# Attention of a fused two-layer kernel: the query norm as a row of the band, squares summed by feature, short products in one group

## The chip, the cores and the metric

The kernel runs on one core of one Trainium2 chip. The metric is the device time of one execution in microseconds. The engines are named as the profile names them: PE (TensorE, matmul), PEld (its weight load), DVE (VectorE), ACT (ScalarE), POOL (GpSimd) and SP (SyncE, which here only issues transfers). SBUF is the working memory, PSUM the eight banks into which PE writes, DRAM the memory off the core.

## The reference, cut to what matters

Four sub-layers over 4 x 512 tokens of width 512 (pooled attention, dense FFN, lag attention, experts), each followed by a layer norm. The change touches only the third, lag attention with 16 heads of 128:

```python
q, k, v = _silu(x @ Wq), _silu(x @ Wk), _silu(x @ Wv);  z = x @ Wz;  a = x @ Wa;  b = x @ Wb
q, k, v = (_causal_dwconv(t, conv) for t in (q, k, v))          # 4 taps along the sequence
q = q * cos + rot_half(q) * sin;  k = k * cos + rot_half(k) * sin
q = q / max(norm(q), 1e-12);  k = k / max(norm(k), 1e-12)       # per token and head
for s in range(4):                                              # lags 0 to 3
    attn = sum(q * lag(k, s)) * scale;  gate = sigmoid(lag(a, s) * b)
    out = out + (attn * gate) * lag(v, s)
rms = rsqrt(mean(out * out over all heads) + EPS)               # per token
out = out * rms * norm_w * _silu(z);  return out @ Wout
```

The norm of q is one factor per token and head. It can be applied to the scores, or, since it is linear, as late as the output's rows. All products are made in float32 by parts: a high part and a low part, three matmuls for one (`product`, lines 45 to 47).

## The kernel before, in words

The lag attention is a software pipeline of 64 steps, one for each head and batch (step s: head s // 4, batch s % 4). Every slot of the loop works on step f (the newest), l1, l2 and l3 (one, two and three steps older). There is no scheduler: the code of each engine is written out by hand, in the order in which it runs, and semaphores (`wait_ge`, `until`) tie the engines together. `BAND` is 131 columns: a tile of 128 keys and the 3 queries behind it.

In one slot PE makes four projections of 12 matmuls each (q and k mixed by halves into A and B, v into A, z into B), the output projection of l2 (4 tiles of 3 matmuls), and five groups of four short ones: it turns the convolved values (`turn_values`, into bank T), makes the scores (`score`, rot_k against rot_q over the band, into S), the mixture (`mix`, values against prob, into O), turns the mixture (`turn_mixed`, into T) and turns the squares of q and k (`turn_tiles(S1, squares[0])`). The short ones stand in two places: values and scores before the first half of the output projection, the other three before its second half.

DVE makes the convolutions (`tap`, three for each of c1, c2, cv), the rotation (cross1, cross2, r1, r2), the sums of squares per token (line 3405), `gains` (gate + 1, times the constant band matrix), `probabilities` (gate times scores), `gated_output`, `y_low` and `accumulate` (adds an output tile to the row in x_tok, times the query norm `rnorm`). ACT makes silu, the zeroth taps, squares, the gates (tanh), the values scaled by the key norm, and `sum_squares` (squares of the turned mixture, summed by the accumulator, times the query norm). POOL makes c1 * cos, c2 * cos, the sum of the two squares, the power -1/2 of the norms (line 3017) and, in three of four slots, the low parts of the next head's weights (`split_head`, lines 2885 and 2888: two of them, two, one). SP issues the gate row (line 2012), the next head's weights, and the four transfers that move the halves of r1 and r2 to rot_q and rot_k (lines 2098 to 2102), which `score` waits for a slot later.

Of the kernel before, what the change touches and what calls it, by code (L numbers as in the profile page):

```python
# [15 lines left out]
P = 128  # L16
# [1766 lines left out]
class Step:  # L1783


    def __init__(self, s):
        self.s, self.head, self.b = s, s // BATCH, s % BATCH
        self.wbuf, self.ybuf, self.rbuf = self.head % 2, s % 2, s % 4


def layers(nc, mem, a, lag_b, saved, store):
# [16 lines left out]
    with phase(nc) as ctx:  # L1808
# [19 lines left out]
        raw1 = overlay("second", [(None, 3 * MAT, F32), ("raw1", 8 * Paired.BLOCK, F32)])["raw1"]  # L1828
        exact = overlay("exact", [(None, 3 * MAT, F32), ("n40", 2 * SEQ, F32), (None, 4 * MAT - 2 * SEQ, F32), ("n41", 2 * SEQ, F32)])
# [6 lines left out]
        lag_a, ssum, expert_weight = small("lag_a", NTT * HEADS), small("ssum", NTT * HEADS), small("expert_weight", NTT * EXPERTS)  # L1836
# [11 lines left out]
        with ExitStack() as room:  # L1848
# [17 lines left out]
                      + [("gate", TPB * BAND, F32), ("mixed", SEQ, F32), ("prob", TPB * BAND, F32),  # L1866
                         ("rot_q", SEQ + PAD, F32), ("values", SEQ, F32), (None, 3 * SEQ - 2 * TPB * BAND - PAD, F32),
                         ("zs", SEQ, F32), ("wo_hi1", HID, F32R), ("wo_lo1", HID, F32R), ("b_row", SEQ + PAD, F32),
                         ("band", BAND, F32), ("conv", HEADS * 3 * LAGS, F32), ("norm", HEADS, F32),
                         ("norm2", 2 * TPB, F32)] + [(f"rnorm{r}", 2 * TPB, F32) for r in range(4)])  # L1870
# [46 lines left out]
        gate, mixed, prob, rot_q, values = banded(lag["gate"]), lag["mixed"], banded(lag["prob"]), lag["rot_q"], lag["values"]  # L1917
        b_row, zs, band_t, conv_t, norm_t = (lag[n] for n in ("b_row", "zs", "band", "conv", "norm"))
        norm2, rnorm = lag["norm2"], [lag[f"rnorm{r}"] for r in range(4)]
# [49 lines left out]
        s_cos, s_cross = sem("cos"), sem("cross")  # L1969
        s_r1, s_r2 = sem("r1"), sem("r2")  # L1970
        s_move1, s_move2 = sem("move1"), sem("move2")
        s_sqr, s_pair = sem("sqr"), sem("pair")
        s_nrm, s_sum, s_n2, s_rn = sem("nrm"), sem("sum"), sem("n2"), sem("rn")
        s_b, s_gate, s_gain = sem("b"), sem("gate"), sem("gain")
        s_s, s_prob = sem("s"), sem("prob")
        s_vt, s_val = sem("vt"), sem("val")
        s_o, s_mix, s_ot, s_osq = sem("o"), sem("mix"), sem("ot"), sem("osq")
        s_y, s_yhi, s_ylo = sem("y"), sem("yhi"), sem("ylo")
# [17 lines left out]
        SWITCH = END - 2  # L1996
# [3 lines left out]
        with nc.Block() as block:  # L2000
            @block.sync
            def _(sp):
# [7 lines left out]
                def factor_row(st):  # L2010
                    row = st.head + HEADS
                    sp.dma_start(b_row[:, 0:SEQ], lag_b[row:row + 1, st.b * SEQ:(st.b + 1) * SEQ]
                                 .to_broadcast([P, SEQ])).then_inc(s_b, 16)

# [53 lines left out]
                save(1)  # L2068
                factors.store(sp, 0)
# [3 lines left out]
                for f, l1, l2, l3 in slots():  # L2073
# [6 lines left out]
                    factor_row(f)  # L2080
                    if f.b == 0:
# [5 lines left out]
                    if f.s == END - 1:  # L2087
                        sp.wait_ge(s_save, BATCH * 16)
                        sp.wait_ge(s_op, (STEPS - BATCH) * TPB)
                        load_residual(0)  # L2090
# [5 lines left out]
                    sp.wait_ge(s_r1, f.s + 1)  # L2096
# [3 lines left out]
                    sp.wait_ge(s_r2, f.s + 1)  # L2100
# [36 lines left out]
            def _(pe):  # L2137
# [5 lines left out]
                def out_projection(st, tiles):  # L2143
# [3 lines left out]
                    for t in tiles:  # L2147
                        until(pe, s_acc, st.s * TPB + t - 1)
                        tok = slice(t * P, (t + 1) * P)
                        product(pe, OP[t % 2], [(y_hi[st.ybuf][:, tok], y_lo[st.ybuf][:, tok])],  # L2150
                                [(wo_hi[st.wbuf], wo_lo[st.wbuf])]).then_inc(s_op, 1)

                def score(st):
                    pe.wait_ge(s_move1, st.s * 32 + 32)
                    pe.wait_ge(s_move2, st.s * 32 + 32)
                    pe.wait_ge(s_sum, st.s + 1)
                    until(pe, s_prob, st.s)
# [5 lines left out]
                def mix(st):  # L2163
                    pe.wait_ge(s_prob, st.s + 1)
# [12 lines left out]

                def turn_values(st):
                    pe.wait_ge(s_cv, st.s * TAPS + TAPS)
                    until(pe, s_osq, st.s - 1 if st.s < SWITCH else st.s)  # L2180
                    turn_tiles(T, cv, s_vt)

                def turn_mixed(st):

                    pe.wait_ge(s_val, st.s + 2)
                    pe.wait_ge(s_mix, st.s + 1)
                    turn_tiles(T, mixed, s_ot)
# [94 lines left out]
                for f, l1, l2, l3 in slots():  # L2282
# [18 lines left out]
                    if l1:  # L2301
# [1358 lines left out]
```

## Time and profile before

| what | value |
|---|---|
| time, median of 3 runs | 2850.29 us (2849.97 to 2850.31) |
| profiled execution, first to last instruction | 2847.8 us (its own time is not recorded beside the span) |
| PE, PEld busy | 2826.6 us (99%), 2348.4 us (82%) |
| DVE busy | 2252.7 us (79%) |
| ACT, POOL busy | 1528.7 us (54%), 1443.2 us (51%) |
| granted TensorE clock, mean | 0.999 of full speed |
| transfers, mean | 56 GB/s |
| chain that ended last, PE's share | 32%, the rest in smaller pieces of other lines |

The span of the profiled execution lies 2.5 us under the median of the timed runs. A slot of the lag attention takes 16.8 us, and the loop of 64 slots lies between about 760 and 1850 us of the span. PE is busy nearly all the time in every stage; DVE is busy nine tenths of the time in the lag attention and less elsewhere. Busy time says what an engine does, not what it waits for; a timeline of one slot tells both.

### The profile page before, as it was taken

How to read it: one execution, taken by the hardware profiler on the slowest of the kernel's cores; microseconds unless marked ns; L12 is line 12 of the kernel's file. 1: busy time of each engine (PE TensorE's matmuls, PEld its weight loads, DVE VectorE, ACT ScalarE, POOL GpSimd, SP SyncE). 2: the span in 40 equal slices, each digit the busy share in tenths (PEclk: the TensorE clock that was granted, in tenths of full speed). 3: DMA queues.
4: the chain of work that ended last, by engine and by line, in shares of the span. 5: the costliest groups of instructions: out<-in, count | busy, mean ns of one | idle time of the engine just before them, and what ended most of it. 6: DMA issues, size and time to landing. Idle time of an engine off the chain costs nothing. (4 is left out here: it accounts for less than half of the span.)

```text
span 2847.8 us, 40066 instructions
## 1 busy us (share of the span) xinstructions
PE 2826.6 (99%) x13466; PEld 2348.4 (82%) x13466; DVE 2252.7 (79%) x3265; ACT 1528.7 (54%) x3149; POOL 1443.2 (51%) x1016
## 2 busy tenths in 40 slices
PE   9999999999999999999999999999999999999998
PEld 7888888888788888888888888778778887888887
DVE  7899587777888889888988898977667677666665
ACT  6656333333666666666666666765545445444443
POOL 7787233334344444444444444666545556555554
PEclk9999999999999999999999999999999999999999
DMA  3000000000322222222222221321111111211111
GB/s 138 1 23 25 12 19 27 30 27 23 125 65 68 70 64 64 65 73 64 64 64 72 77 71 53 93 75 52 52 45 52 60 45 56 86 45 60 52 52 45
DMA packets 79099, 160.44 MB, mean 56 GB/s; under 512 B 11313, under 2 KB 19889, under 8 KB 77873
## 3 DMA queue, kind: packets, MB, share of 16 engines
q1 hardware_dynamic: 78896, 157.88, 18.5%
q8 instruction: 110, 1.80, 0.3%
q14 instruction: 93, 0.75, 0.1%
HBM read 115.63 MB, written 8.65 MB: 44 GB/s over the span
## 5 line engine op out<-in xcount | busy, mean ns | idle before, releaser
L1546 DVE SCALAR_TENSOR_TENSOR x_tok<-OP,expert_weight,x_tok 128x512 f32<-128x512 f32 x252 | 188.1, 748 | 138.2 <-PE OP L47 138.1
L1425 POOL TENSOR_TENSOR middle_w_lo<-second_raw,middle_w_hi 128x512 fp32r<-128x512 f32 (+1 forms) x96 | 143.4, 1496 | 208.7 <-ACT middle_w_hi L1420 208.7
L1518 POOL TENSOR_TENSOR middle_in_lo<-middle_slot,middle_in_hi 128x512 fp32r<-128x512 f32 x128 | 168.6, 1318 | 131.7 <-ACT middle_in_hi L1514 130.9
L3017 POOL TENSOR_TENSOR lag_rnorm<-lag_norm,minus_half 128x8 f32<-128x8 f32 x64 | 105.1, 1643 | 209.5 <-DVE lag_norm L3408 209.5
L45 PE MATMUL B<-xT_hi,lag_w_hi 128*128 128x512 f32 x516 | 201.4, 390 | 1.8 <-DVE xT_lo L496 1.5
L47 PE MATMUL B<-xT_hi,lag_w_lo 128*128 128x512 f32 x516 | 201.6, 391 | 0.0
L45 PE MATMUL A<-xT_hi,lag_w_hi 128*128 128x512 f32 x512 | 200.6, 392 | 0.4 <-DVE xT_lo L496 0.4
L46 PE MATMUL B<-xT_lo,lag_w_hi 128*128 128x512 f32 x516 | 200.8, 389 | 0.0
L47 PE MATMUL A<-xT_hi,lag_w_lo 128*128 128x512 f32 x512 | 199.9, 390 | 0.0
L46 PE MATMUL A<-xT_lo,lag_w_hi 128*128 128x512 f32 x512 | 199.4, 389 | 0.0
L45 PE MATMUL OP<-middle_down_hi,middle_in_hi 128*128 128x512 f32 x496 | 193.6, 390 | 1.9 <-POOL middle_down_lo L1445 1.7
L47 PE MATMUL OP<-middle_down_hi,middle_in_lo 128*128 128x512 f32 x496 | 193.0, 389 | 0.0
L46 PE MATMUL OP<-middle_down_lo,middle_in_hi 128*128 128x512 f32 x496 | 193.0, 389 | 0.0
L3086 DVE SCALAR_TENSOR_TENSOR lag_c<-A,lag_conv,lag_c 128x511 f32<-128x511 f32 (+2 forms) x192 | 143.8, 749 | 60.4 <-ACT lag_c L2694 55.9
L1425 POOL TENSOR_TENSOR middle_w_lo<-middle_raw,middle_w_hi 128x512 fp32r<-128x512 f32 (+1 forms) x96 | 154.4, 1613 | 64.6 <-ACT middle_w_hi L1420 62.6
L3097 DVE SCALAR_TENSOR_TENSOR x_tok<-OP,lag_rnorm,x_tok 128x512 f32<-128x512 f32 x240 | 173.5, 744 | 2.9 <-PE OP L47 2.9
L1263 DVE TENSOR_TENSOR x_tok<-OP,x_tok 128x512 f32<-128x512 f32 x188 | 128.8, 688 | 54.7 <-PE OP L47 54.3
L3086 DVE SCALAR_TENSOR_TENSOR lag_c<-B,lag_conv,lag_c 128x511 f32<-128x511 f32 (+2 forms) x192 | 143.4, 747 | 25.2 <-ACT lag_c L2702 23.0
L3013 POOL TENSOR_TENSOR lag_r<-lag_c,lag_cos 128x512 f32<-128x512 f32 x64 | 83.5, 1305 | 155.4 <-DVE lag_c L3086 155.4
L3008 POOL TENSOR_TENSOR lag_r<-lag_c,lag_cos 128x512 f32<-128x512 f32 x64 | 83.0, 1296 | 153.1 <-DVE lag_c L3086 153.1
L1508 ACT ACTIVATE middle_slot<-middle_slot 128x512 f32<-128x512 f32 x128 | 80.8, 632 | 139.2 <-DVE middle_slot L1527 139.1
L3086 DVE SCALAR_TENSOR_TENSOR lag_cv<-A,lag_conv,lag_cv 128x511 f32<-128x511 f32 (+2 forms) x192 | 143.7, 748 | 12.8 <-ACT lag_cv L2720 2.0
(670 smaller groups left out, 9103.8 us busy)
## 6 DMA issues: line engine op xcount, KB each, us to landing
lag_raw<-in_head_weights SPq DMA_DIRECT2D x64, 256.0 KB, 4.5
lag_b_row<-lag_b_scratch SPq DMA_DIRECT2D x64, 256.0 KB, 3.3
lag_rot_q<-lag_r SPq DMA_DIRECT2D x128, 128.0 KB, 2.3
lag_rot_k<-lag_r SPq DMA_DIRECT2D x128, 128.0 KB, 2.4
middle_down_raw<-in_expert_down SPq DMA_DIRECT2D x32, 512.0 KB, 3.4
middle_raw<-in_expert_in SPq DMA_DIRECT2D x32, 384.0 KB, 3.0
second_raw<-in_expert_in SPq DMA_DIRECT2D x32, 384.0 KB, 3.0
double_raw<-in_dense_in SPq DMA_DIRECT2D x12, 512.0 KB, 3.4
```

What stands on the lines that cost most here:

```text
L45: pe.matmul(out, lh, rh, start=first and k == 0, stop=False)
L46: pe.matmul(out, lh, rl, start=False, stop=False)
L47: done = pe.matmul(out, ll, rh, start=False, stop=last and k == n - 1)
L1263: dve.tensor_tensor(row, self.down_bank(q, n), row, ALU.add).then_inc(self.s_acc, 1)
L1425: pool.tensor_tensor(self.w_lo[q % 2][:, out], self.raw[q % 2][:, of], f32(self.w_hi[q % 2][:, out]), ALU.subtract).then_inc(self.s_wlo, 1)
L1518: pool.tensor_tensor(self.inner_lo[q % 3][t], self.slot((1, 3)[t], q), f32(self.inner_hi[q % 3][t]), ALU.subtract).then_inc(self.s_lo, 1)
L1546: dve.scalar_tensor_tensor(row, self.down_bank(v, n), self.expert_weight[:, e:e + 1], row, op0=ALU.mult, op1=ALU.add).then_inc(self.s_acc, 1)
L3008: pool.tensor_tensor(r1, c1, cos, ALU.mult).then_inc(s_cos, 1)
L3013: pool.tensor_tensor(r2, c2, cos, ALU.mult).then_inc(s_cos, 1)
L3017: pool.tensor_tensor(rnorm[f.rbuf], norm2, half[:, 0:2 * TPB], ALU.pow).then_inc(s_rn, 1)
L3086: dve.scalar_tensor_tensor(out[:, shift:], src[:, 0:SEQ - shift], wj, out[:, shift:], op0=ALU.mult, op1=ALU.add).then_inc(done, 1)
L3097: dve.scalar_tensor_tensor(row, OP[t % 2], at(rnorm[st.rbuf], 2 * t), row, op0=ALU.mult, op1=ALU.add).then_inc(s_acc, 1)
```

## The change

The query norm no longer scales the output rows, it scales the probabilities. The norms of a step lie with tokens in partitions (128 x 8). DVE turns them in blocks of 32x32 (`turn_norms`), five small stores write them to DRAM as a row for each tile (`store_query`), one load spreads the row over all partitions (`load_query`, 128x524), POOL multiplies it by the band matrix (`band_of_query`), and `probabilities` multiplies the gate by that. `gains` now takes the scores from PSUM in place of the band. The probabilities and `mix` are made one slot later (for l2), `accumulate` is a plain add, the power on POOL stands ahead of c1 * cos.

The turned mixture and `sum_squares` are gone but for the last two steps. ACT squares the mixture as it takes it from PSUM (`mixture`, Square), POOL adds it by an accumulating transfer into DRAM, one region per batch (`add_squares`), and PE turns each region once at the end (`turn_sums`). PE makes all short products of a slot in one group (squares, values, mixture, scores) and all four tiles of the output projection behind one another, into OP0, OP1, S0 and S1. The turned squares go to OP1.

```diff
+                def store_query(st):
+                    sp.wait_ge(s_n2, 3 * st.s + 3)
+                    until(sp, s_query, st.s * 96)
+                    window = query_norm[st.s % 2, :, :]
+                    for g in range(TPB):
+                        sp.dma_start(window[:, g * 32:(g + 1) * 32], turned[g * 32:g * 32 + TPB, :]).then_inc(s_query, 16)
+                    sp.dma_start(window[0:TPB - 1, P:BAND], turned[1:TPB, 0:PAD]).then_inc(s_query, 16)
+
+                def load_query(st):
+                    sp.wait_ge(s_query, st.s * 96 + 80)
+                    until(sp, s_prob, 2 * st.s)
+                    sp.dma_start(lag["query"], query_norm[st.s % 2:st.s % 2 + 1, :, :].rearrange("a t n -> a (t n)")
+                                 .to_broadcast([P, TPB * BAND])).then_inc(s_query, 16)
...
                     if l1:
+                        turn_squares(l1)
                         turn_values(l1)
+                        if l2:
+                            mix(l2)
                         score(l1)
-                    if l2:
-                        if l2.s == 0:
-                            pe.wait_ge(factors.s_c, BATCH)
-                        out_projection(l2, (0, 1))
...
                         projection(l1, 3, B, s_z)
-                        if f.s < SWITCH:
-                            if l2:
-                                turn_mixed(l2)
-                            mix(l1)
...
-                    turn_tiles(S1, squares[0], s_nrm)
...
+                    if l2:
...
+                        out_projection(l2, range(TPB), [OP0, OP1, S0, S1], 4)
...
+                def band_of_query(st):
+                    pool.wait_ge(s_query, st.s * 96 + 96)
+                    pool.tensor_tensor(query[:, :, :], query[:, :, :], band_t.unsqueeze(1).to_broadcast([P, TPB, BAND]),
+                                       ALU.mult).then_inc(s_band, 1)
+
+                def add_squares(st):
+                    pool.wait_ge(s_mix, st.s + 1)
+                    if st.s < WHOLE:
+                        until(pool, s_squares, st.s * 16)
+                        sums = square_sums[st.b * P:(st.b + 1) * P, :]
+                        if st.head:
+                            pool.dma_start(sums, head_out[st.s], accum_op=ALU.add).then_inc(s_squares, 16)
...
                 def gains(st):
                     dve.wait_ge(s_gate, st.s + 1)
-                    dve.scalar_tensor_tensor(gate[:, :, :], gate[:, :, :], 1.0,
-                                             band_t.unsqueeze(1).to_broadcast([P, TPB, BAND]),
-                                             op0=ALU.add, op1=ALU.mult).then_inc(s_gain, 1)
+                    dve.wait_ge(s_s, st.s + 1)
+                    dve.scalar_tensor_tensor(gate[:, :, :], gate[:, :, :], 1.0, scores[:, :, 0:BAND],
+                                             op0=ALU.add, op1=ALU.mult).then_inc(s_prob, 1)
 
                 def probabilities(st):
-                    dve.wait_ge(s_s, st.s + 1)
-                    dve.wait_ge(s_gain, st.s + 1)
+                    dve.wait_ge(s_prob, 2 * st.s + 1)
                     until(dve, s_o, st.s)
-                    dve.tensor_tensor(prob[:, :, :], gate[:, :, :], scores[:, :, 0:BAND], ALU.mult).then_inc(s_prob, 1)
+                    if st.s < BY_ROW:
+                        dve.wait_ge(s_band, st.s + 1 + (st.s > WHOLE))
+                        dve.tensor_tensor(prob[:, :, :], gate[:, :, :], query[:, :, :], ALU.mult).then_inc(s_prob, 1)
...
+                def turn_norms(st):
+                    dve.wait_ge(s_rn, st.s + 1)
+                    until(dve, s_query, st.s * 96)
+                    dve.transpose(turned, norms[st.rbuf]).then_inc(s_n2, 1)
```

On PE, in the middle of the loop, the short products of one slot. Before, from the end of the z projection on (`lag_mixed` is the mixture, `lag_cv` the values, `lag_square` the squares):

```order
L47 MATMUL B<-xT_hi,lag_w_lo 128x512
L2175 MATMUL T<-ident,lag_mixed 128x128 x4
L2169 MATMUL O<-lag_prob,lag_values 128x131 x3
L2169 MATMUL O<-lag_prob,lag_values 128x128
L2175 MATMUL S<-ident,lag_square 128x128 x4
```

and now, between the second and the third projection:

```order
L47 MATMUL B<-xT_hi,lag_w_lo 128x512
L2216 MATMUL OP<-ident,lag_square 128x128 x4
L2216 MATMUL T<-ident,lag_cv 128x128 x4
L2210 MATMUL O<-lag_prob,lag_values 128x131 x3
L2210 MATMUL O<-lag_prob,lag_values 128x128
L2200 MATMUL S<-lag_rot_q,lag_rot_k 128x131 x4
L45 MATMUL A<-xT_hi,lag_w_hi 128x512
```

The turned mixture is gone, and the values and scores, which had a place of their own, stand in the same group.

On POOL, one slot of the loop with weight splits. Before:

```order
L2885 TENSOR_TENSOR lag_w_lo<-lag_raw,lag_w_hi 128x512 x2
L3008 TENSOR_TENSOR lag_r<-lag_c,lag_cos 128x512
L3013 TENSOR_TENSOR lag_r<-lag_c,lag_cos 128x512
L3015 TENSOR_TENSOR lag_square<-lag_square 128x512
L3017 TENSOR_TENSOR lag_rnorm<-lag_norm,minus_half 128x8
```

and now (`square_sums_scratch` is the region in DRAM to which the mixture's squares are added; the slot shown is one with a single split):

```order
L2952 TENSOR_TENSOR lag_query<-lag_query,lag_band 128x524
L2944 TENSOR_TENSOR lag_w_lo<-lag_raw,lag_w_hi 128x512
L3082 TENSOR_TENSOR lag_norms<-lag_norm,minus_half 128x8
L3085 TENSOR_TENSOR lag_r<-lag_c,lag_cos 128x512
L2961 DMA square_sums_scratch<-head_squares 128x512
L3090 TENSOR_TENSOR lag_r<-lag_c,lag_cos 128x512
L3092 TENSOR_TENSOR lag_square<-lag_square 128x512
```

The band product and the issue of the transfer are new, and the power has moved from the end to the front, so that c1 * cos comes after it.

On DVE, the part of a slot from the sums of squares to the rotation, as it stands now (before, each cross product stood directly behind the convolution or the probabilities, and the sums of squares at the end of the slot):

```order
L3214 TENSOR_REDUCE lag_norm<-OP 128x4x2
L3217 TENSOR_SCALAR lag_norm<-lag_norm 128x8
L3167 SCALAR_TENSOR_TENSOR lag_c<-B,lag_conv,lag_c 128x511
L3204 SCALAR_TENSOR_TENSOR O<-O,lag_norm,lag_zs 128x512
L3167 SCALAR_TENSOR_TENSOR lag_c<-B,lag_conv,lag_c 128x510
L3167 SCALAR_TENSOR_TENSOR lag_c<-B,lag_conv,lag_c 128x509
L3188 SCALAR_TENSOR_TENSOR lag_gate<-lag_gate,S 128x524
L3222 STREAM_TRANSPOSE lag_turned<-lag_norms 128x32
L3209 TENSOR_TENSOR lag_y_lo<-O,lag_y_hi 128x512
L3480 TENSOR_TENSOR lag_cross<-lag_c,lag_sin 128x512
L3486 TENSOR_TENSOR lag_cross<-lag_c,lag_sin 128x512
```

Both cross products stand together now, behind the turn of the norms and y_low.

## Rows read from the trace of the kernel before

**Rows 1.** Windows; us, then busy time of each engine, clock, DMA share, GB/s

```profile
800.00:1780.00 980.00, 980.00 (x5139) 833.44 (x5138) 877.43 (x1343) 624.59 (x1643) 416.95 (x305) 1.00 0.25 67
1780.00:1880.00 100.00, 97.96 (x486) 76.07 (x485) 84.87 (x141) 74.11 (x178) 59.34 (x52) 1.00 0.31 93
```

**Rows 2.** Timeline of PE in one slot; start, us, line, out<-in, count

```profile
1105.89 0.60 PE L2175 MATMUL T<-ident,lag_mixed 128*128 128x128 f32 x4
1106.33 1.06 PE L2169 MATMUL O<-lag_prob,lag_values 128*128 128x131 f32 x8
1107.23 0.60 PE L2175 MATMUL S<-ident,lag_square 128*128 128x128 f32 x4
1107.58 0.48 PE L45 MATMUL OP<-lag_w_hi,lag_y_hi 128*128 128x512 f32 x1
...
1114.48 0.60 PE L2175 MATMUL T<-ident,lag_cv 128*128 128x128 f32 x4
1114.92 1.06 PE L2159 MATMUL S<-lag_rot_q,lag_rot_k 128*128 128x131 f32 x8
1115.74 0.48 PE L45 MATMUL OP<-lag_w_hi,lag_y_hi 128*128 128x512 f32 x1
1116.05 0.40 PE L46 MATMUL OP<-lag_w_lo,lag_y_hi 128*128 128x512 f32 x1
...
1122.65 0.60 PE L2175 MATMUL T<-ident,lag_mixed 128*128 128x128 f32 x4
```

**Rows 3.** Timeline of DVE in the same slot; idle time before, in brackets

```profile
1108.19 0.75 DVE L3115 SCALAR_TENSOR_TENSOR O<-O,lag_norm,lag_zs 128x512 f32<-128x512 f32 x1
1108.85 0.68 DVE L3405 TENSOR_REDUCE lag_norm<-S 128x8 f32<-128x512 f32 x1
1109.57 0.17 DVE L3408 TENSOR_SCALAR lag_norm<-lag_norm 128x8 f32<-128x8 f32 x1
...
1113.44 2.32 DVE L3086 SCALAR_TENSOR_TENSOR lag_c<-A,lag_conv,lag_c 128x511 f32<-128x511 f32 x3 [0.87 <-ACT lag_c L2694]
1116.10 0.75 DVE L3086 SCALAR_TENSOR_TENSOR lag_c<-B,lag_conv,lag_c 128x511 f32<-128x511 f32 x1 [0.35 <-ACT lag_c L2702]
1116.77 0.69 DVE L3110 TENSOR_TENSOR lag_prob<-lag_gate,S 128x524 f32<-128x524 f32 x1
1117.37 0.69 DVE L3360 TENSOR_TENSOR lag_cross<-lag_c,lag_sin 128x512 f32<-128x512 f32 x1
1117.97 1.53 DVE L3086 SCALAR_TENSOR_TENSOR lag_c<-B,lag_conv,lag_c 128x510 f32<-128x510 f32 x2
1119.42 1.40 DVE L3097 SCALAR_TENSOR_TENSOR x_tok<-OP,lag_rnorm,x_tok 128x512 f32<-128x512 f32 x2
...
1121.52 2.32 DVE L3086 SCALAR_TENSOR_TENSOR lag_cv<-A,lag_conv,lag_cv 128x511 f32<-128x511 f32 x3
1123.75 0.68 DVE L3394 TENSOR_TENSOR lag_r<-lag_r,lag_cross 128x512 f32<-128x512 f32 x1
```

**Rows 4.** Timeline of POOL in the same slot

```profile
1109.82 1.65 POOL L3017 TENSOR_TENSOR lag_rnorm<-lag_norm,minus_half 128x8 f32<-128x8 f32 x1 [3.21 <-DVE lag_norm L3408]
1111.67 2.63 POOL L2885 TENSOR_TENSOR lag_w_lo<-lag_raw,lag_w_hi 128x512 fp32r<-128x512 f32 x2 [0.21 <-ACT lag_w_hi L2442]
```

**Rows 5.** Tile view, expert stage; durations in ns, min/median/max

```profile
L1537 DVE TENSOR_TENSOR middle_slot<-middle_slot x64: 682/1762/1773, 1880.5 to 2827.5; 128x512 f32<-128x512 f32 x64
```

**Rows 6.** Timeline of POOL, expert stage

```profile
1897.95 1.41 POOL L1518 TENSOR_TENSOR middle_in_lo<-middle_slot,middle_in_hi 128x512 fp32r<-128x512 f32 x1 [1.30 <-ACT middle_in_hi L1514]
```

**Rows 7.** Timeline of DVE, same place

```profile
1898.24 1.40 DVE L1406 TENSOR_TENSOR middle_raw<-middle_raw 128x256 f32<-128x256 f32 x1
```

**Rows 8.** SP's issues of the gate row; ns each, min/median/max

```profile
L2012 SPq DMA_DIRECT2D lag_b_row<-lag_b_scratch x64: 325/332/585, 765.1 to 1819.4; - x64
```

**Rows 9.** Transfers of 1060 to 1160 us; count, KB, median us from issue to landing

```profile
lag_b_row<-lag_b_scratch SPq DMA_DIRECT2D x6, 256.0 KB, 3.2
```

**Rows 10.** The four 64 KB stores into lag_b_scratch, issue to landing

```profile
DMA to landing us min/median/max: 1.6/2.7/3.5
```

More of the change, by code:

```diff
@@ L1828, in layers @@
         raw1 = overlay("second", [(None, 3 * MAT, F32), ("raw1", 8 * Paired.BLOCK, F32)])["raw1"]
+        of_batch = overlay("sums", [(None, MAT, F32)] + [(f"rows{b}", SEQ, F32) for b in range(BATCH)])
         exact = overlay("exact", [(None, 3 * MAT, F32), ("n40", 2 * SEQ, F32), (None, 4 * MAT - 2 * SEQ, F32), ("n41", 2 * SEQ, F32)])
@@ L1916, in layers @@
         c1, c2, cv, rot_k, squares = lag["c1"], lag["c2"], lag["cv"], lag["rot_k"], [lag["square0"], lag["square1"]]
-        gate, mixed, prob, rot_q, values = banded(lag["gate"]), lag["mixed"], banded(lag["prob"]), lag["rot_q"], lag["values"]
+        gate, prob, rot_q, values = banded(lag["gate"]), banded(lag["prob"]), lag["rot_q"], lag["values"]
+        query = banded(lag["query"])
+        sum_rows = [of_batch[f"rows{b}"] for b in range(BATCH)]
+        head_out = {**{s: head_squares for s in range(STEPS - 3)}, END - 2: lag["query"][:, 0:SEQ],
+                    END - 1: lag["query"][:, 0:SEQ], END: squares[1]}
         b_row, zs, band_t, conv_t, norm_t = (lag[n] for n in ("b_row", "zs", "band", "conv", "norm"))
-        norm2, rnorm = lag["norm2"], [lag[f"rnorm{r}"] for r in range(4)]
+        norm2, norms, turned = lag["norm2"], [lag["norms0"], lag["norms1"]], lag["turned"]
         residual = [[middle[f"res{g}{t}"] for t in range(TPB)] for g in range(BATCH)]
@@ L1977, in layers @@
         s_o, s_mix, s_ot, s_osq = sem("o"), sem("mix"), sem("ot"), sem("osq")
+        s_query, s_band = sem("query"), sem("band")
+        s_squares, s_rows = sem("squares"), sem("rows")
         s_y, s_yhi, s_ylo = sem("y"), sem("yhi"), sem("ylo")
@@ L2760, in _ @@
                 rows.high_tile(act, 3)
+                mixture(last_step)
                 rows.copy(act, 0)
@@ L3355, in _ @@
                         norm1.aggregate(dve, 3)
+                    if l2:
+                        gated_output(l2)
+                    tap(1, f, B, c2, 2, s_c2)
+                    tap(1, f, B, c2, 3, s_c2)
+                    if l1:
+                        gains(l1)
+                        if f.s == END:
+                            probabilities(l1)
+                            sum_features(2, OP0)
+                        turn_norms(l1)
+                    if f.s == 1:
+                        factors.take(dve, 3, 3)
@@ L3356, in _ @@
+                    if l2:
+                        y_low(l2)
                     dve.wait_ge(s_c1, f.s * TAPS + TAPS)
[L3357 removed]
+                    until(dve, s_rotated, 4 * f.s)
                     if f.s == 0:
                         dve.wait_ge(s_rotation, 32)
[L3360 to L3363 removed]
@@ L3385, in _ @@
+                    until(dve, s_rotated, 4 * f.s - 1)
+                    dve.tensor_tensor(cross1, c2, sin, ALU.mult).then_inc(s_rotated, 1)
+                    dve.wait_ge(s_tap, f.s * 3 + 3)
+                    tap(2, f, A, cv, 1, s_cv)
                     tap(2, f, A, cv, 2, s_cv)
@@ L3427, in _ @@
                 accumulate(before_last, 1)
-                rows.low_tile(dve, 0)
-                for t in (1, 2, 3):
+                for t in range(TPB):
                     rows.low_tile(dve, t)
```

357 lines of the change are left out of this document (195 added, 162 removed).

## The prediction

> **What bounds the kernel now.** I read the windows first. In the loop of the lag attention PE is busy 980.00 of 980 us at full clock, DVE 877.43, ACT and POOL far less [rows 1]. So PE sets the time, and what counts is how far apart its instructions start. The timeline of PE shows that: one slot runs from 1105.89 to 1122.65, 16.76 us [rows 2]. From 1116.05 to the next turned mixture stand 29 wide matmuls in 6.60 us, 0.228 each. Four turns cost 0.44 us behind a wide matmul (1105.89 to 1106.33) and 0.35 behind short ones (1107.23 to 1107.58); the mixture costs 0.90, the scores 0.82, and the first wide matmul behind a short group 0.31 in place of 0.228 [rows 2].
>
> The timeline of DVE shows how near the next bound is. By the starts, a tensor_tensor takes 0.60 us, the gated output 0.66, the sums of squares 0.72, three convolution taps 2.23, two of them 1.45, one 0.67; the idle pieces of 0.87 and 0.35 are waits for ACT [rows 3]. DVE rests under 2 us in a slot.
>
> **PE's part.** Before, the short work is 0.44 + 0.90 + 0.35 + 0.08 and 0.44 + 0.82 + 0.08 = 3.11 us a slot. Now it is one group: squares 0.44, values 0.35, mixture 0.90, scores 0.82, and 0.08 behind it, 2.59. PE needs 16.24 us a slot, 0.52 less: 0.35 is the turned mixture, the rest is the second entry and exit. Some 60 slots have the whole pattern: 31 us, if nobody makes PE wait.
>
> **DVE's part.** I write one slot from the start of the probabilities, with the durations of [rows 3]. Probabilities 0 to 0.60; taps of c1 to 2.83; sums of squares to 3.55; maximum 0.17, to 3.72; a tap of c2 to 4.39; gated output to 5.05; two taps to 6.50; gains, now with PSUM, 0.65, to 7.15; the 32x32 turn, which no row shows, between the 0.17 of the smallest instruction and 0.60 of a 512-wide one: 128x32 is nearest to 0.17, to 7.32; y_low to 7.93; cross2 to 8.53; cross1 to 9.13; cv to 11.36; r1, r2 to 12.56; four accumulates, plain adds now, at 0.60 in place of about 0.66 (1119.42 to the next cross product is 1.32 for two), to 14.96. Sum 15.0 against PE's 16.24: free, by itself.
>
> **Who blocks whom.** In the expert stage a DVE product of two SBUF tiles takes 0.68 us at best and 1.76 in the median [rows 5]: it stands still while POOL runs. A POOL product takes 1.31 alone (2.63 for two, [rows 4]). At 1897.95 one takes 1.41, and the DVE product issued behind it at 1898.24 takes 1.40 although it is half as wide as the other, whose least is 0.68 [rows 6, 7]. I read this as an exclusive right, given in the order of asking, for a whole instruction. In the loop before the cross products show none of it (0.69, [rows 3]): no POOL product runs there. The Trainium skill states the same limit ("SBUF — State Buffer", Who interferes with whom): only a DVE instruction with two SBUF inputs meets a POOL instruction that reads SBUF, one with a PSUM input does not. By that rule, with which the stretched rows agree, the probabilities are newly exposed: gate times scores read PSUM, gate times query reads SBUF twice.
>
> *Cross products.* POOL starts the power 0.08 behind the maximum, at 3.80, ends it at 5.45 (1.65, [rows 4]), makes c1 * cos to 6.75, issues the adding transfer, and makes c2 * cos and the sum of squares. No row shows a transfer that POOL issues. From below: what SP takes for one, 0.33 to 0.59 [rows 8]. From above: 2.6, two POOL products. The nearest rows for something POOL has to work out for 128 partitions are its product, 1.31, and its power, 1.65 [rows 4]; I take 1.3 to 1.65. Then c2 * cos asks between 8.05 and 8.40, while cross2 (7.93 to 8.53) runs; it gets the port at 8.53, and cross1 waits until 9.84. Cost 1.3 us; DVE's slot is 16.3. The thresholds: under 1.18 us c2 * cos comes ahead of cross2, and both cross products are held (1.4 to 2.5 us); over 1.78 neither, at most 0.4. The Trainium skill gives about 1 us to the first byte for a transfer issued by POOL ("DMA: Bandwidth & Descriptors", Specifications); no run here shows it. As an estimate by that page the issue would fall under the threshold, with the time of the second rival below.
>
> *Probabilities.* SP sees the turned norms at 7.35. Five small stores start 0.37 to 0.63 apart (issue 0.33 to 0.59 [rows 8] and 0.04 between); at 0.45 the last starts at 9.15. The four 64 KB stores landed in 1.6 to 3.5 us, median 2.7 [rows 10]; here it is under 0.6 KB, so I take 1.6: 10.75. SP is blocked meanwhile; behind it wait the moves of r1 and r2, which are ready only past 12, so this costs nothing. The load is of the gate row's shape, 3.2 us [rows 9]: 13.98. Band product 1.31: 15.34 with the signals. POOL goes straight on to its weight splits in three of four slots, 1.31 each [rows 4], two, two and one. DVE asks at 16.3, the first split ends at 16.65: 0.35 us in three slots of four, 0.26 on average. The slot is 16.56.
>
> So PE waits for DVE (the third projection for c2, the first of the next slot for cv), and of its 0.52 us 0.20 remain: 12 us over 60 slots.
>
> **The rest.** ACT loses the turned squares and gains nothing; it rests anyway [rows 1]. The adding transfer has a slot to land. The end of the loop gets four sums of 512 columns by feature on DVE (0.68 each, the duration in [rows 3], 2.7 us), four turned regions on PE (0.44 each) and their loads; PE rests 2.04 us there now [rows 1]. Between 0 and 8 us lost; I take 2, since the other work there covers part.
>
> **Sum.** The profiled execution's span is 2847.8 us; 12 less and 2 more make 2837.8, and with the 2.5 us by which the median of the runs lies above that span, 2840. 0.2% is 5.7 us, what a measurement of this kernel can tell from no change.
>
> **Rivals.**
>
> *PE stays the bound.* The issue on POOL lasts past 1.78 us, or the held products fall into DVE's slack, and the row comes in time. Against it: the probabilities wait for the band at 15.34 and are held by a split. Even then DVE's slot is at most 16.65 in three slots and 15.34 in one, 16.3 on average, PE's 16.24. For it: PE never waits today. 0.46 to 0.52 us by 60 less 2 us: 2821 to 2825.
>
> *Slower: both cross products held.* The issue on POOL takes under 1.18 us, say 0.7. c2 * cos takes the port at 7.45, cross2 waits to 8.76, the sum of squares asks meanwhile and goes ahead of cross1: 2.1 us a slot, DVE at 17.1; the second split (16.65 to 17.96) holds the probabilities for 0.86 us in two slots of four. 17.5 against 16.76: 46 us more, 2896 to 2898. It decides from 1.18 us down. For it: SP's 0.33 to 0.59. Against it: POOL's own rows.
>
> *Slower: the row is late.* At a landing of 2.7 and 0.6 between the stores the band product ends at 17.0, a split holds the probabilities to 18.3 in three slots of four: 18.0 on average, 1.24 by 60, 75 us, and half of that at half the delay; 2889 to 2927.
>
> *The sizes cancel.* A collision a little larger, or an end 5 us dearer: within 0.2%.
>
> **Chances.** Forecast 0.35, of which 0.30 lie below 2844.6 and 0.05 within 0.2%; its own range is 2828 to 2850. PE bound 0.24. Both held 0.23. Row late 0.10. Cancelled 0.08. So faster 0.54, same 0.13, slower 0.33. The range goes from 2820, under the first rival, to 2898, which leaves out most of the late row and little more.
>
> **What would show it.** PE: the turned mixtures gone, one group of 16 short products in about 2.5 us; its idle time before the third projection and before the first, put down to taps on DVE. DVE: cross1 near 1.9 us and cross2 near 0.69 is my forecast; both long is the slower rival; both 0.69 the faster. Probabilities near 1.0 us where splits follow, 0.69 in every fourth slot. POOL: the space between c1 * cos and c2 * cos is the issue. SP: five stores, then the load; if DVE's idle time ahead of the probabilities is put down to the band product, the late row decides. I am wrong if DVE's slot is not the sum of these, or if PE waits for a move or the gate instead.

## The result, and the profile after

The changed kernel takes 2918.9 us (median of 4 runs, 2917.2 to 2920.1) against 2850.3: 1.024 of the time before, 95% interval 1.0226 to 1.0254. It is 2.4% slower. I had forecast 2840, with 0.33 for slower, and the time lies outside my range as well.

The page of the changed kernel (busy time and share; then groups: busy us, mean ns | idle time before them):

```profile
PE 2824.5 (97%) x13234; PEld 2324.3 (80%) x13234; DVE 2393.1 (82%) x3332; ACT 1449.4 (50%) x2653; POOL 1586.8 (54%) x1140
L45 PE MATMUL A<-xT_hi,lag_w_hi 128*128 128x512 f32 x512 | 211.6, 413 | 61.7 <-DVE lag_cv L3167 61.3
```

Its windows, as in [rows 1], and two from the end of the loop:

```profile
800.00:1780.00 980.00, 924.80 (x4655) 764.63 (x4653) 955.01 (x1330) 524.29 (x1124) 522.94 (x403) 1.00 0.40 94
1890.00:1900.00 10.00, 5.32 (x24) 4.58 (x22) 9.93 (x22) 2.25 (x6) 1.99 (x2) 0.64 0.59 159
1900.00:1910.00 10.00, 7.29 (x29) 5.98 (x30) 5.89 (x11) 7.03 (x14) 8.80 (x9) 0.67 0.18 53
```

The bound has changed hands: DVE is busy 955 of 980 us, and PE, which never waited in [rows 1], rests 55 us, 48 of them ahead of the first projection, until the last tap of cv is made. The mean slot is 17.68 us, where it was 16.81 (60 slots each, from the first silu of the second step to that of the 62nd). The last step starts 53.5 us later than before; the other 15.7 us of the profiled difference (span 2917.0 against 2847.8) lie behind that start, 13.4 of them ahead of the first matmul of the experts.

The timeline of DVE in one slot, to be read beside [rows 3]:

```profile
1206.31 0.17 DVE L3217 TENSOR_SCALAR lag_norm<-lag_norm 128x8 f32<-128x8 f32 x1
1209.76 0.20 DVE L3222 STREAM_TRANSPOSE lag_turned<-lag_norms 128x32 f32<-128x32 f32 x1
1209.89 0.65 DVE L3209 TENSOR_TENSOR lag_y_lo<-O,lag_y_hi 128x512 fp32r<-128x512 f32 x1
1210.46 3.01 DVE L3480 TENSOR_TENSOR lag_cross<-lag_c,lag_sin 128x512 f32<-128x512 f32 x1
1213.39 0.68 DVE L3486 TENSOR_TENSOR lag_cross<-lag_c,lag_sin 128x512 f32<-128x512 f32 x1
1213.99 2.31 DVE L3167 SCALAR_TENSOR_TENSOR lag_cv<-A,lag_conv,lag_cv 128x511 f32<-128x511 f32 x3
1219.81 1.83 DVE L3196 TENSOR_TENSOR lag_prob<-lag_gate,lag_query 128x524 f32<-128x524 f32 x1
```

and that of POOL:

```profile
1206.56 1.67 POOL L3082 TENSOR_TENSOR lag_norms<-lag_norm,minus_half 128x8 f32<-128x8 f32 x1 [3.67 <-DVE lag_norm L3217]
1208.21 1.28 POOL L3085 TENSOR_TENSOR lag_r<-lag_c,lag_cos 128x512 f32<-128x512 f32 x1
1209.45 0.88 POOL L2961 DMA_DIRECT2D square_sums_scratch<-head_squares  x1
1210.10 1.56 POOL L3090 TENSOR_TENSOR lag_r<-lag_c,lag_cos 128x512 f32<-128x512 f32 x1
1211.36 1.54 POOL L3092 TENSOR_TENSOR lag_square<-lag_square 128x512 f32<-128x512 f32 x1
1217.28 1.29 POOL L2952 TENSOR_TENSOR lag_query<-lag_query,lag_band 128x524 f32<-128x524 f32 x1 [4.37 <-DMA lag_query<-query_norm_scratch]
```

I read the record of a held product as running from where its engine asks for it to its end. cross2 is asked at 1210.46 and ends 0.6 us after the sum of squares does, although that sum starts 0.90 us later than cross2 asks; cross1 behind it is free. The issue of the transfer keeps POOL for 0.65 us (1209.45 to 1210.10), and the two products behind it are recorded 0.3 us into one another. Over 50 slots (ns, least/median/most):

```profile
L3480 DVE TENSOR_TENSOR lag_cross<-lag_c,lag_sin x50: 2546/2942/3034, 911.0 to 1775.3; 128x512 f32<-128x512 f32 x50
L3486 DVE TENSOR_TENSOR lag_cross<-lag_c,lag_sin x50: 676/679/683, 913.9 to 1778.2; 128x512 f32<-128x512 f32 x50
L3196 DVE TENSOR_TENSOR lag_prob<-lag_gate,lag_query x50: 696/699/1839, 902.8 to 1766.5; 128x524 f32<-128x524 f32 x50
```

Of these 50 probabilities 10 are held for a whole product of POOL (1.13 us), 6 more for under 0.5 us. The slot's sum: from one start of the probabilities to the next 18.20 us here, less the two holds (3.01 - 0.68 and 1.84 - 0.70) leave 14.73 of DVE's own. Over the 60 slots cross2's mean hold is 2.23 us and that of the probabilities 0.28, and DVE rests 0.48; together 17.72, against 17.68 measured.

### The profile page after: what moved, and what is told of

Read it like the earlier page. It is cut to its first block, busy times and chain, and to the rows that moved or that the text cites. A ratio compares the mean times of both kernels' runs of the same rounds, so it can differ in the third digit from the quotient of the medians.

```text
span 2917.0 us, 39883 instructions
## 1 busy us (share of the span) xinstructions
PE 2824.5 (97%) x13234; PEld 2324.3 (80%) x13234; DVE 2393.1 (82%) x3332; ACT 1449.4 (50%) x2653; POOL 1586.8 (54%) x1140
## 3 DMA queue, kind: packets, MB, share of 16 engines
q8 instruction: 108, 1.77, 0.3%
## 4 chain that ended last, share of the span: by engine, by line
PE 60%; DVE 29%; issue 6%; ACT 3%; DMA 1%; POOL 1%; SPq 0%; DVEq 0%; ACTq 0%; POOLq 0%
PE OP L45 7%; PE OP L47 6%; PE OP L46 6%; DVE lag_c L3167 6%; DVE lag_cross L3480 6%; DVE lag_cv L3167 4%; PE S L1470 3%; PE S L1472 3%; PE S L1471 3%; PE A L45 2%; PE A L1470 2%; PE A L1472 2%; PE A L1471 2%; PE A L47 2%; PE A L46 2%
## 5 line engine op out<-in xcount | busy, mean ns | idle before, releaser
L45 PE MATMUL A<-xT_hi,lag_w_hi 128*128 128x512 f32 x512 | 211.6, 413 | 61.7 <-DVE lag_cv L3167 61.3
L3082 POOL TENSOR_TENSOR lag_norms<-lag_norm,minus_half 128x8 f32<-128x8 f32 x63 | 105.0, 1667 | 244.3 <-DVE lag_norm L3217 244.3
L2952 POOL TENSOR_TENSOR lag_query<-lag_query,lag_band 128x524 f32<-128x524 f32 x62 | 84.6, 1364 | 263.6 <-DMA lag_query<-query_norm_scratch 263.6
L2748 ACT ACTIVATE A<-A 128x512 f32<-128x512 f32 x64 | 37.2, 582 | 342.1 <-PE A L47 342.1
L3480 DVE TENSOR_TENSOR lag_cross<-lag_c,lag_sin 128x512 f32<-128x512 f32 x64 | 179.5, 2804 | 0.0
L45 PEld LDWEIGHTS A<-xT_hi,lag_w_hi 128*128 128x128 f32 x512 | 96.0, 188 | 103.4 <-DVE lag_cv L3167 62.8
L1470 PE MATMUL S<-xT_hi,middle_w_hi 128*128 128x512 f32 x384 | 150.4, 392 | 1.5 <-ACT middle_slot L1503 0.8
```

The source lines that it names most:

```text
L45: pe.matmul(out, lh, rh, start=first and k == 0, stop=False)
L1470: pe.matmul(out, w_hi, hi[:, k, :], start=first and k == 0, stop=False, skip_group_check=not first)
L3480: dve.tensor_tensor(cross2, c1, sin, ALU.mult).then_inc(s_rotated, 1)
```

## The experiments

My theory after the result: the holds of cross2 and of the probabilities by POOL, and nothing of the row's way through DRAM, cost the loop its 53.5 us, and the end is a cost of its own. The rivals: the row is late, or the transfers' own traffic slows DVE. Ten kernels followed.

| kernel | cross2, cross1 (median us) | mean slot | time, us | against before, 95% |
|---|---|---|---|---|
| before | 0.69, 0.69 | 16.81 | 2850.3 | |
| after | 2.94, 0.68 | 17.68 | 2918.9 | 1.0226 to 1.0254 |
| x1, no row | 3.91, 1.77 | 20.75 | 3103.8 | 1.0875 to 1.0907 |
| x2, products wait | 0.68, 0.68 | 16.77 | 2862.7 | 1.0025 to 1.0053 |
| x3, splits wait too | 0.68, 0.68 | 16.36 | 2838.9 | 0.9947 to 0.9973 |
| x4, transfer last | 0.77, 1.77 | 16.62 | 2854.0 | 1.0003 to 1.0022 |
| x5, x3 and the end | as x3 | 16.42 | 2839.1 | 0.9951 to 0.9976 |
| x6, only splits wait | 2.92, 0.68 | 17.56 | 2909.0 | 1.0194 to 1.0222 |
| x7, x4 and splits wait | 0.76, 1.78 | 16.50 | 2847.3 | 0.9981 to 0.9999 |
| x8, y_low later | 3.48, 0.68 | 19.94 | 3055.4 | 1.0703 to 1.0735 |
| x9, pause for transfer | 1.50, 1.78 | 17.49 | 2910.1 | 1.0194 to 1.0229 |
| x10, transfer first | 3.00, 0.68 | 18.15 | 2949.6 | 1.0334 to 1.0369 |

**x1.** SP's stores and load are gone, and POOL's band product multiplies band by band, so it waits for nothing; the norms are left out of the result.

```diff
-                        store_query(l1)
-                        load_query(l1)
...
-                    pool.wait_ge(s_query, st.s * 96 + 96)
-                    pool.tensor_tensor(query[:, :, :], query[:, :, :], band_t.unsqueeze(1).to_broadcast([P, TPB, BAND]),
+                    until(pool, s_prob, 2 * st.s)
+                    pool.tensor_tensor(query[:, :, :], band_t.unsqueeze(1).to_broadcast([P, TPB, BAND]), band_t.unsqueeze(1).to_broadcast([P, TPB, BAND]),
```

> The five stores of the norms as a row and the load that spreads them are left out, and the band product multiplies the band by itself, so the query norm is missing from the output; all else stands. Theory A (the SBUF port: cross2 is held 2.3 us behind two POOL products, DVE's own work of 15.0 us and this hold set the slot): the slot stays near 17.3 us, cross2 near 2.9 us, the probabilities go to 0.69 us everywhere since the weight splits are over by then; 2895 to 2905 us. Theory B (the row's way through DRAM sets the slot): without it the slot falls to PE's 16.24 us, and the time to about 2835 us.

3103.8 us: both missed. Without the wait for the row, POOL runs from the transfer through three products without a break. POOL, and the cross product under it, in one slot:

```profile
1317.50 0.89 POOL L2959 DMA_DIRECT2D square_sums_scratch<-head_squares  x1
1318.16 1.56 POOL L3088 TENSOR_TENSOR lag_r<-lag_c,lag_cos 128x512 f32<-128x512 f32 x1
1319.41 1.55 POOL L3090 TENSOR_TENSOR lag_square<-lag_square 128x512 f32<-128x512 f32 x1
1320.65 1.32 POOL L2950 TENSOR_TENSOR lag_query<-lag_band 128x524 f32<-128x524 f32 x1
```

```profile
1318.60 3.93 DVE L3477 TENSOR_TENSOR lag_cross<-lag_c,lag_sin 128x512 f32<-128x512 f32 x1
```

cross2 is held over all three. In 29 of 43 slots a weight split stands behind the band product, but starts 0.03 to 0.4 us after its end; there DVE got its turn first, and cross1, asked behind that, was held by the split (1.77 us). In one slot POOL asked for the split 0.21 us before the band product ended, and cross2 was held over four products, with cross1 free (0.68):

```profile
1716.39 1.30 POOL L2950 TENSOR_TENSOR lag_query<-lag_band 128x524 f32<-128x524 f32 x1
1717.48 1.45 POOL L2941 TENSOR_TENSOR lag_w_lo<-lag_raw,lag_w_hi 128x512 fp32r<-128x512 f32 x1
```

```profile
1714.24 5.26 DVE L3477 TENSOR_TENSOR lag_cross<-lag_c,lag_sin 128x512 f32<-128x512 f32 x1
```

PE waits 1.4 to 3.4 us a slot, and its granted clock falls to a mean of 0.91 between 1000 and 1600 us, which makes the slot longer still. The wait for the row had been a shield: it kept the band product off the rotation.

**x2 and x3.** POOL's second product waits for both cross products; in x3 the weight splits also wait for the probabilities.

```diff
                     until(pool, s_move2, f.s * 32)
+                    pool.wait_ge(s_rotated, 4 * f.s + 2)
                     pool.tensor_tensor(r2, c2, cos, ALU.mult)
...
+                        if l2 and l2.s < BY_ROW:
+                            pool.wait_ge(s_prob, 2 * l2.s + 2)
                         split_head(f.head + 1, 1 - f.wbuf, SPLIT_AT[f.b])
```

> One wait more: POOL starts c2 * cos only when DVE has made both cross products. The adding transfer and its traffic stay. Theory A (port): cross2 falls from 2.9 to 0.69 us, the slot from 17.6 to about 16.9 us, because now the row's way binds (15.9 us from turn to turn, and 1.15 us more where a weight split holds the probabilities, in three slots of four); about 2874 us. Rival C (the cross product is slowed by the transfer that POOL issues just ahead of it, not by POOL's products): cross2 stays near 2.9 us and the time near 2919 us.

> The wait of x2, and a second: POOL starts the weight splits only when DVE has made the probabilities. Theory A: no two-input DVE product meets a POOL product any more except perhaps r1; probabilities and cross products near 0.69 us, the slot 16.24 us, bound by PE as counted in the prediction; about 2835 us with the dearer end of the loop (16 us) as it is in the changed kernel. Theory B (late row): the slot stays over 16.8 us and DVE rests ahead of the probabilities, 2870 us or more.

x2 takes 56 us off (2862.7, where 2874 was expected), and x3 another 24 (2838.9, against 2835), which is 0.4% under the kernel before, with all of the change in it. Both transfers are still there, so traffic on them isn't what made cross2 long. x3's cross2 and probabilities, and its short products on PE, which answer to [rows 2]:

```profile
L3483 DVE TENSOR_TENSOR lag_cross<-lag_c,lag_sin x54: 678/681/685, 899.5 to 1765.5; 128x512 f32<-128x512 f32 x54
L3199 DVE TENSOR_TENSOR lag_prob<-lag_gate,lag_query x54: 703/705/2215, 907.7 to 1774.5; 128x524 f32<-128x524 f32 x54
```

```profile
1219.98 0.60 PE L2216 MATMUL OP<-ident,lag_square 128*128 128x128 f32 x4
1220.42 0.60 PE L2216 MATMUL T<-ident,lag_cv 128*128 128x128 f32 x4
1220.86 1.06 PE L2210 MATMUL O<-lag_prob,lag_values 128*128 128x131 f32 x8
1221.75 1.06 PE L2200 MATMUL S<-lag_rot_q,lag_rot_k 128*128 128x131 f32 x8
1222.57 0.47 PE L45 MATMUL A<-xT_hi,lag_w_hi 128*128 128x512 f32 x1
```

0.44 + 0.44 + 0.89 + 0.82, and 0.08 in the first wide one: 2.67, where I had 2.59 (the values cost 0.44, not 0.35). PE is busy 979.44 of 980 us, the slot is 16.36. One product is still held, r1 by POOL's sum of squares (1.14 us in the median), and PE doesn't wait for it.

**x4.** The adding transfer is issued behind the sum of squares (`add_squares(l2)` moves two instructions down).

> Only the place of the adding transfer changes: POOL issues it behind the sum of the squares and no longer between c1 * cos and c2 * cos, so both products come 0.65 us earlier. If the port is given in the order of asking: cross2 near 0.8 us, cross1 near 2.0 us. If POOL keeps it for as long as its next product is ready: cross2 near 2.1 us, cross1 0.69. If the products overlapped by 0.3 us only because they stood behind the transfer, they go back from 1.56 to 1.29 us each. In all three cases the hold falls from 2.3 to about 1.4 us, the slot to about 16.9, the time to about 2875 us.

2854.0 us, where I had 2875. cross2, cross1, and POOL's sum of squares:

```profile
L3480 DVE TENSOR_TENSOR lag_cross<-lag_c,lag_sin x53: 709/765/867, 902.9 to 1764.2; 128x512 f32<-128x512 f32 x53
L3486 DVE TENSOR_TENSOR lag_cross<-lag_c,lag_sin x53: 1769/1774/1780, 903.6 to 1764.9; 128x512 f32<-128x512 f32 x53
L3090 POOL TENSOR_TENSOR lag_square<-lag_square x53: 1728/1732/1737, 903.1 to 1764.4; 128x512 f32<-128x512 f32 x53
```

Here the engines do take turns: cross2 goes behind c2 * cos, the sum of squares waits 0.44 for it, and cross1 waits for the sum. But two things had changed at once, what stood ahead of the products and the moment at which DVE asked. x8 to x10 separate them.

**x5.** x3 with the work behind the loop in another order.

```diff
+                    if f.s == END:
+                        accumulate(third, 0)
+                        accumulate(third, 1)
                     if f.s >= END - 1:
                         mean_squares(f.s - (END - 1))
...
-                for t in range(TPB):
-                    accumulate(third, t)
-                y_low(before_last)
+                accumulate(third, 2)
+                accumulate(third, 3)
                 statistics(0)
                 norm_2.aggregate(dve, 0)
                 norm_sums(last_step)
+                y_low(before_last)
                 sum_features(3, OP0)
...
-                pool.wait_ge(s_n2, 3 * END + 2)
-                pool.tensor_tensor(norms[last_step.rbuf][:, 0:2 * TPB], norm2, half[:, 0:2 * TPB], ALU.pow).then_inc(s_rn, 1)
                 mean_root(1)
                 norm_2.root(pool, 0)
+                pool.wait_ge(s_n2, 3 * END + 2)
+                pool.tensor_tensor(norms[last_step.rbuf][:, 0:2 * TPB], norm2, half[:, 0:2 * TPB], ALU.pow).then_inc(s_rn, 1)
```

> The version with both waits (2838.9 us), with the work behind the last step put in another order: DVE takes the third-last step's first two output tiles into the rows ahead of the two sums of the rotation, the statistics of the first rows ahead of the norm sums, and the last low half behind them; POOL takes the two small powers of the statistics ahead of the power of the last norm. Theory (the 14.5 us behind the last step are PE's four waits of 1.1, 2.6, 2.7 and 2.5 us there and the lower clock that follows on them): the second and third wait shrink by 3 to 5 us together, and if the clock stays at its high level another 5 to 7 us come back: 2829 to 2834 in all. Rival (the clock falls for another reason, or the waits move on to the next thing that DVE is late with): 2836 to 2839.

2839.1, no gain over x3. PE's longest waits there, x3 first, then x5 (sum, times, longest):

```profile
PE OP L45 <- DVE lag_norm L3220: 2.7, 1, 2.7
PE OP L2216 <- DVE x_tok L3182: 2.6, 1, 2.6
```

```profile
PE S L2200 <- DMA lag_rot_k<-lag_r: 3.1, 1, 3.1
PE OP L45 <- DVE ms L3229: 2.9, 1, 2.9
```

x3's third wait, 2.5 us ahead of the turns of x_tok (L945), is gone in x5. The others moved on: the accumulates ahead of the rotation's sums made these late, and the scores wait for their move. The clock still falls, for a shorter time: by the granted clock of 10 us rows, 13.6 us at the 1.2 GHz level in x3 (0.73 and 0.59 from 1810 to 1830) and 6.8 in x5 (0.66 from 1820 to 1830). From the last step's start to the end it is 1039.7 us in place of 1043.2 (before: 1028.6), but in this profiled execution that start is 4.9 us later, in steps whose order is the same in both; why, no run shows. For the time the rival holds.

**x6 and x7.** The splits' wait alone, in the changed kernel and in x4.

> The changed kernel with one wait alone: POOL begins the weight splits only when DVE has the product of gate and band (probabilities). The products of the rotation stay as they are. If the two costs add (both waits took 24 us more than the wait for the cross products alone): the probabilities at 0.70 us in every slot, cross2 still held at about 3 us, the slot about 17.35, and 2893 to 2900. Rival (the time saved at the probabilities is lost again at the cross products, as DVE then meets POOL at another moment): 2910 to 2919.

> The adding transfer behind the sum of squares, and the wait of the splits for the probabilities. cross2 at 0.7 to 0.87 us, cross1 held 1.1 us (one POOL product), the probabilities at 0.70. DVE's own work of 15.0 us and 1.2 us held give 16.2, at PE's 16.24, so PE is the bound: 2839 to 2845. Rival (the hold of cross1 comes ahead of the cv taps that PE waits for, and PE loses part of it each slot): about 2850.

x6 2909.0, x7 2847.3, both between my two readings. The probabilities are free in x6 (0.69 us in every slot), yet this gives 10 us and not 24. Two reasons are in the traces. They were held for a whole product in only 10 of 50 slots of the changed kernel, but in 39 of 52 of x2 (1.67 us in the median): with cross2 held, DVE comes later to the splits. And DVE's sum isn't the whole bound: in x6's slot at 1209 us the last tap of cv ends at 1212.65, PE makes the first projection, ACT silu and scale, and the taps of c1 start at 1217.24. That round takes 4.6 us, and DVE has 4.2 us of work for it, so a hold there is partly free.

**x8.** DVE's y_low goes behind both cross products, so that cross2 is asked 0.57 us earlier.

> The changed kernel with one DVE instruction moved: the low half of y (reads PSUM, 0.6 us) goes behind both cross products, from the third step on, so cross2 asks about 0.57 us earlier, some 0.2 us before POOL begins c2 * cos. If the right is given in the order of asking, cross2 takes 0.68 to 0.75 us, c2 * cos waits for it, and cross1, asked while c2 * cos runs, is held once (1.3 to 1.9 us in all): the slot loses about 1.2 us of its 17.6, 2845 to 2865. If what is held is held over both POOL products whenever they follow one another, cross1 takes 2.4 to 3.0 us, and the time is 2895 to 2919.

3055.4: both missed. POOL and then cross2 in one slot:

```profile
1217.73 0.87 POOL L2961 DMA_DIRECT2D square_sums_scratch<-head_squares  x1
1218.38 1.54 POOL L3090 TENSOR_TENSOR lag_r<-lag_c,lag_cos 128x512 f32<-128x512 f32 x1
1219.64 1.53 POOL L3092 TENSOR_TENSOR lag_square<-lag_square 128x512 f32<-128x512 f32 x1
```

```profile
1218.26 3.46 DVE L3480 TENSOR_TENSOR lag_cross<-lag_c,lag_sin 128x512 f32<-128x512 f32 x1
```

cross2 asks 0.12 us ahead of c2 * cos, while the transfer is being issued, and stands behind both products all the same. The order of asking is refuted here: 0.12 us is little where POOL's records overlap by 0.3, but the sum of squares starts 1.38 us after cross2 has asked and still goes first, as it did in the changed kernel. The time is more than this hold: y_low now starts 4.0 us later in DVE's order (cross1 and the held cross2), PE waits 2.0 to 2.4 us a slot for it ahead of the output products, and its mean clock over the span falls to 0.969.

**x9.** x4 with a power of two columns on POOL where the transfer had been.

```diff
                     if l2 and l2.s < BY_ROW:
-                        add_squares(l2)
+                        pool.wait_ge(s_rn, l1.s + 1)
+                        pool.tensor_tensor(pause, norms[l1.rbuf][:, 0:2], half[:, 0:2], ALU.pow)
```

> The version with the adding transfer last (2854.0 us), and in the place where the transfer was a power of two columns, which should take POOL about 0.65 us, as the transfer did. DVE then asks for cross2 some 0.3 to 0.4 us after c2 * cos has begun, as in the changed kernel, but with no transfer ahead. If the moment of asking decides (a DVE product asked in the first part of one of two POOL products in a row is held over both), cross2 takes 2.5 to 3.0 us and cross1 0.68, and the time is 2900 to 2919. If the transfer ahead decides, DVE gets the turn behind c2 * cos: cross2 1.2 to 1.8, cross1 1.2 to 1.8, the sum of squares longer, 2870 to 2905.

```profile
L3089 POOL TENSOR_TENSOR pause<-lag_norms,minus_half x50: 693/694/697, 908.4 to 1763.4; 128x2 f32<-128x2 f32 x50
L3484 DVE TENSOR_TENSOR lag_cross<-lag_c,lag_sin x50: 1410/1500/1527, 909.4 to 1764.5; 128x512 f32<-128x512 f32 x50
L3490 DVE TENSOR_TENSOR lag_cross<-lag_c,lag_sin x50: 1770/1776/1784, 910.9 to 1765.9; 128x512 f32<-128x512 f32 x50
L3094 POOL TENSOR_TENSOR lag_square<-lag_square x50: 1728/1734/1741, 910.4 to 1765.4; 128x512 f32<-128x512 f32 x50
```

The pause takes the transfer's time to 0.03 us, DVE asks at the same point of c2 * cos (0.42 us behind its start, 0.36 in the changed kernel), and now the turns alternate: cross2 waits for one product, the sum of squares for cross2, cross1 for the sum. What stands ahead decides, not the moment. The durations are those of my second reading, but not its time (2870 to 2905): the two holds of 1.9 us together cost almost what 2.26 did, 2910.1, which lies in the range of the first. The durations tell the mechanisms apart, the time would not have.

**x10.** The transfer one place earlier, behind the power and ahead of c1 * cos.

> The changed kernel with the adding transfer one place earlier: behind the power and ahead of c1 * cos, so three POOL products follow it instead of two. cross2 is asked at the same place of DVE's order, when POOL is near the end of c2 * cos or at the sum of squares (as in the version with the transfer last, where it took 0.76 us and cross1 1.77). If POOL keeps the right from the transfer on through every product that follows without a break, the products are recorded 0.3 us into one another (1.54 to 1.57 us each), cross2 is held until the sum of squares ends, 1.5 to 2.5 us, and cross1 takes 0.68: 2875 to 2919. If the transfer spoils only the next change of turn, POOL and DVE alternate again: cross2 up to 1.4, cross1 1.77, POOL's sum of squares 1.73, 2880 to 2910 with the later start. The durations tell the two apart, not the time.

POOL and cross2 in one slot:

```profile
1219.19 0.89 POOL L2961 DMA_DIRECT2D square_sums_scratch<-head_squares  x1
1219.84 1.57 POOL L3087 TENSOR_TENSOR lag_r<-lag_c,lag_cos 128x512 f32<-128x512 f32 x1
1221.10 1.56 POOL L3090 TENSOR_TENSOR lag_r<-lag_c,lag_cos 128x512 f32<-128x512 f32 x1
1222.35 1.55 POOL L3092 TENSOR_TENSOR lag_square<-lag_square 128x512 f32<-128x512 f32 x1
```

```profile
1221.45 3.01 DVE L3480 TENSOR_TENSOR lag_cross<-lag_c,lag_sin 128x512 f32<-128x512 f32 x1
```

2949.6 us. Of what I wrote for the first reading POOL's durations and the free cross1 came out; cross2 is longer (3.0 us, not 1.5 to 2.5), and so is the time: cross2 is asked only 0.35 us into the second product and ends 0.6 us behind the third. Three products stand 0.3 us into one another. So POOL keeps the right from the transfer through the products that follow without a break, and x1's slots show how little of a break is enough: 0.03 us ahead of the fourth product gave DVE its turn, and with no break cross2 was held over four. x8 and the changed kernel say the same, and x4 and x9, with no transfer ahead, alternate, though their products too follow at a pitch of 1.25. Why a transfer ahead makes the difference stays open.

## Why the prediction was wrong

The forecast was 79 us off: the loop at +53.5 us in place of -12, and the end at +15.7 in place of +2.

**PE's part: right.** I had 0.52 us a slot and a slot of 16.24 if nobody makes PE wait. x3 measures 16.36, and the missing 0.12 is mostly the values at 0.44.

**DVE's own work: right.** 15.0 us against 14.73. The bound isn't its sum alone, as x6 shows, but that moved little.

**The issue on POOL: wrong, and the first step to fail.** I took 1.3 to 1.65 us by the nearest rows of POOL's own work and set SP's 0.33 to 0.59 [rows 8] aside; it is 0.65. The two kinds of work have nothing in common but the engine, while SP's row is of the same act. My own threshold of 1.18 then gives the second rival: both cross products late by 2.1 us, slot 17.5. Measured: 2.26 and 17.68. That rival's 2896 to 2898 is still 21 us short, of which 14 are the end. The rule of the Trainium skill that I set beside it ("DMA: Bandwidth & Descriptors", Specifications, about 1 us to the first byte) pointed the right way, though no run here shows a first byte; here the transfer's issue and its landing are different things, the second 4.1 us in the median behind the first.

**"In the order of asking": wrong.** The exclusive right itself is shown, by the held durations and by x2 and x3, which take them away. The held ones among DVE's instructions are those that the Trainium skill names ("SBUF — State Buffer", Who interferes with whom), the ones with two SBUF inputs; y_low, with one input in PSUM, takes 0.65 us while c2 * cos starts. The order is not shown: it is refuted. Without a transfer ahead they alternate (x4, x9), behind one POOL keeps it (x1, x8, x10). In the changed kernel both readings give nearly the same hold, 2.1 us split over both cross products or 2.26 on cross2 alone, so that the rival's slot fits is in part luck; I would have mispriced any reordering, as I did with x1 and x8.

**The row: right.** From the end of the turn (1209.96) to the end of the band product (1218.57) it takes 8.6 us; I had 8.0. The turn is 0.20 us, near the 0.17 that I took. PE's waits ahead of the first projection (47.7 us from 900 to 1780) are all put down to cv's taps.

**The probabilities: right in kind.** 0.28 us a slot on average; I had 0.26, from 0.35 us in three slots of four, where it was 1.13 us in one of five and less in a few more. So the average came out by luck. The price depends on where DVE arrives: 39 of 52 slots in x2.

**The end: mis-sized.** I took 2 us of 0 to 8; in the changed kernel and x2 to x5 it is 11 to 16 (x3 14.6). PE's waits in the changed kernel:

```profile
PE OP L2216 <- DVE x_tok L3179: 3.3, 1, 3.3
PE A L945 <- ACT x_tok L586: 2.5, 1, 2.5
PE OP L45 <- DVE lag_norm L3217: 1.6, 1, 1.6
```

7.4 us, where the kernel before had 1.9 from the start of its last step on. From the first of them on the windows at 1890 and 1900 show a granted clock of 0.64 and 0.67, part of them at the 1.2 GHz level, where two wide matmuls start 0.43 us apart in place of 0.23. DVE is busy 9.93 of 10 us there, with sums and statistics that I had counted one by one (2.7 us) but not laid against the wait of each product of PE. x5 shows that the order alone doesn't cure it. The waits make 5.5 us more than before. The two rows hold 13.8 us at the lower level, in which PE can have lost half at most, 6.9 (an estimate); with the four turned regions (0.44 each, as in the prediction) that about fills the 13.4 us ahead of the experts. How much each is worth was not separated by a run, and where the 2 us behind, in the experts, come from stays open.

## What to carry to other kernels

A transfer issued by POOL was cheap for POOL (0.65 us) and dear for DVE (2.26): put it behind POOL's last product before a wait, not ahead of a series. Where DVE bounds, or nearly so, try waits on POOL that let DVE's two-operand SBUF products go first: the two of x3 were worth 80 us here. Before a wait is taken from POOL, look what DVE product its next instructions will then meet: x1 took away a DMA round trip and lost 185 us. And price an unseen instruction by the row of the same act on another engine, not by other acts on its own.

## What the runs showed of the hardware that I had not expected

- POOL's products behind its own transfer last 1.54 to 1.57 us and start 1.25 apart, and DVE gets no turn between, over two products (the changed kernel, x8), three (x1, x10) and once four (x1); with no transfer ahead an unheld one lasts 1.28 with a pitch of 1.25 too, and DVE does get a turn (x4, x9).
- The power of two columns on POOL takes 0.69 us, of eight 1.67: about 0.16 us a column over some 0.37 that doesn't depend on them (an estimate from these two).
- The granted clock follows PE's waits inside the loop: with waits of 1.4 to 3.4 us in each slot of x1 and 2.0 to 2.4 in x8 it fell (0.91 and 0.93 over 1000 to 1600 us), while the waits of up to 1.3 us a slot in the changed kernel left it at 1.00. Behind the loop it fell with a wait of 3.3 us.
